# One-hot counting stage of a graph-attention kernel: register load, negation of x and the two score rows each put at another place

## The reference

```python
HW = h @ W
s = HW @ a[:512, 0];  t = HW @ a[512:, 0]
e = leaky_relu(s[row] + t[col], 0.2)          # row = src, col = dst
m = segment_max(e, row);  ex = exp(e - m[row])
att = ex / segment_sum(ex, row)[row]
agg = segment_sum(att[:, None] * h[col], row)
out = silu(agg) @ base_w.T + einsum(b_splines(agg), spline_w)
x = layernorm(x + out)
```

## The kernel before, in words

| windows | last tile | batch | group |
|---|---|---|---|
| 8, 9 | 67 | 8 | 5 |
| 10, 11 | 81 | 10 | 6 |
| 12, 13 | 94 | 11 | 7 |
| 14, 15 | 107 | 13 | 8 |
| 16, 17 | 121 | 15 | 9 |
| 18, 19 | 134 | 16 | 9 |
| 20, 21 | 147 | 18 | 10 |
| 22; 23; 24 | 153; 160; 166 | 19; 20; 20 | 11; 12; 12 |

## Time and profile before

### The profile page before, as it was taken

How to read it: one execution, slowest core, us unless ns; L and a number is a source line. 1 busy time by engine, 2 the same in 40 slices (tenths; PEclk the granted TensorE clock), 3 DMA queues, 4 the chain that set the end, 5 groups by cost and what they waited for, 6 DMA issues and landing times.

```text
span 384.6 us, 5446 instructions
## 1 busy us (share of the span) xinstructions
PE 370.0 (96%) x2082; PEld 304.6 (79%) x2082; DVE 336.8 (88%) x428; ACT 253.6 (66%) x252; POOL 37.1 (10%) x92
## 2 busy tenths in 40 slices
PE   7797899999999999999999999999999999999994
PEld 3676568888888888888888888888888888888883
DVE  8998799987764889999899997988999799999455
ACT  6769745445337979874876874896766696766122
POOL 6001301000000010101001010100100101010000
PEclk9999999999999999999999999999999999999999
DMA  7911987000000066577644546342343353453102
GB/s 253 399 23 40 221 147 217 2 2 0 2 0 0 2 208 179 168 239 219 179 151 149 180 119 203 117 109 56 114 128 88 104 146 109 154 192 111 55 27 109
DMA packets 23979, 47.28 MB, mean 123 GB/s; under 512 B 1936, under 2 KB 2412, under 8 KB 23954
## 3 DMA queue, kind: packets, MB, share of 16 engines
q0 software_dynamic: 12416, 24.00, 23.7%
q1 hardware_dynamic: 11538, 22.95, 18.4%
HBM read 44.37 MB, written 2.57 MB: 122 GB/s over the span
## 4 chain that ended last, share of the span: by engine, by line
PE 86%; DVE 8%; ACT 2%; issue 2%; POOL 1%; DVEq 1%; POOLq 0%
PE PS L1414 38%; PE PS L1410 25%; PE PS L1351 18%; PE PS L1333 3%; DVE oh L557 2%; DVE still L573 2%; PE PS L1361 1%; ACT C L1045 1%; DVE hit L536 1%; DVE oh L523 1%; ACT Z L1050 1%; PE PS L1424 0%; ACT xl L1055 0%; DVE pat L546 0%; DVEq L301 0%
## 5 line engine op out<-in xcount | busy, mean ns | idle before, releaser
L1414 PE MATMUL PS<-wh,s 128*128 128x512 f32 x432 | 139.4, 390 | 0.0
L1414 PEld LDWEIGHTS PS<-wh,s 128*128 128x128 f32 x432 | 81.2, 188 | 16.8
L1410 PE MATMUL PS<-s,wh 128*128 128x482 f32 x288 | 92.8, 383 | 0.0
L1414 PE MATMUL PS<-wl,s 128*128 128x512 f32 x216 | 84.2, 390 | 0.0
L1144 ACT ACTIVATE s<-v 128x1220 fp32r<-128x1220 f32 (+1 forms) x32 | 40.0, 1251 | 37.5 <-DVE v L932 26.3
L1410 PEld LDWEIGHTS PS<-s,wh 128*128 128x128 f32 x288 | 54.6, 189 | 9.7
L1127 ACT ACTIVATE v<-xt,bias 128x1220 f32<-128x1220 f32 (+1 forms) x32 | 42.9, 1341 | 20.1 <-DVE s L942 18.1
L1410 PE MATMUL PS<-s,wl 128*128 128x482 f32 x144 | 55.2, 384 | 0.0
L926 DVE SCALAR_TENSOR_TENSOR v<-v,v 128x1220 f32<-128x1220 f32 (+1 forms) x32 | 46.4, 1451 | 6.3 <-ACT v L1130 6.3
L932 DVE SCALAR_TENSOR_TENSOR v<-v,v 128x1220 f32<-128x1220 f32 (+1 forms) x32 | 46.8, 1461 | 3.3
L514 POOL DMA_DIRECT2D wh<-in_splT x32 | 23.0, 718 | 256.1 <-PE PS L1414 183.0
(11 more groups left out here) (162 smaller groups left out, 427.3 us busy)
## 6 DMA issues: line engine op xcount, KB each, us to landing
wh<-in_splT POOLq DMA_DIRECT2D x32, 512.0 KB, 4.2
wring<-in_splT SPq DMA_DIRECT2D x21, 512.0 KB, 4.5
xt<-in_xT SPq DMA_DIRECT2D x1, 2500.0 KB, 12.2
xh<-in_x POOLq DMA_DIRECT2D x1, 2304.0 KB, 11.8
wh<-in_baseT POOLq DMA_DIRECT2D x4, 512.0 KB, 5.5
out<-xr SPq DMA_DIRECT2D x8, 256.0 KB
wring<-in_baseT SPq DMA_DIRECT2D x3, 512.0 KB, 4.0
xr<-in_x SPq DMA_DIRECT2D x1, 1280.0 KB, 5.9
```

The lines of the kernel that those rows point to most:

```text
L1410: m = e.matmul(PS[:, w, 0:TURNED], wx[:, ic, 128 * w:128 * w + 128], sx[:, ic, 0:TURNED], start=begins, stop=ends_)
L1414: m = e.matmul(PS[:, out_bank(w), :], sx[:, ic, c:c + 128], wx[:, ic, :], start=begins, stop=ends_)
```

## The change

- `left_table` runs one group later, between `hits(9)` and `one_hot_still(9)`, and not behind `lanes(8)`. `LOADS_AT` becomes 9: DVE's five register loads stand behind the issue of `lanes(9)`, and PE's load behind group 9 and `s_column`.
- `minus_x(k)` runs at the end of batch 7 + k for all ten k.
- PE's `st_rows` parts stand behind groups 3 to 6, ACT's `st_rows` before the evacuation of batch 11.
- ACT's `s_part` stands before the evacuations at batch 17, not at its end.

```diff
-        LOADS_AT = 8
-        NEGATIVE_AT = {11 + k: k for k in range(NT - 3)}
+        LOADS_AT = 9
+        NEGATIVE_AT = {7 + k: k for k in range(NT)}
@@ vector
+                if g == 9:
+                    left_table()
                 one_hot_still(g)
...
-                if g == 8:
-                    left_table()
                 if g == LOADS_AT:
@@ scalar
-                if b == 13:
+                if b == 11:
                     st_rows()
+                if b == 17:
+                    e.wait_ge(s_sc, 4)
+                    for k, (lo, hi) in enumerate(TCH):
+                        e.mul(s_part[:, lo // 128:hi // 128], ...
                 for w, n in TAKEN:
                     if LAST_TILE[w + n - 1] // TB == b:
                         evacuate_counts(w, n)
...
                 if b in NEGATIVE_AT:
                     k = NEGATIVE_AT[b]
                     minus_x(k)
-                if b == 17:
-                    e.wait_ge(s_sc, 4)
-                    (the same s_part lines)
-            for k in range(len(NEGATIVE_AT), NT):
-                minus_x(k)
@@ tensor
-                if g in (4, 5, 6, 7):
-                    st_rows(g - 4)
+                if g in (3, 4, 5, 6):
+                    st_rows(g - 3)
```

More of the change, by code:

```diff
@@ L1061, in _ @@
                            PS[:, 6:8, 0:4].rearrange("p b (a c) -> p a b c", c=2)).then_inc(s_wa, 1)
-                if b == 13:
+                if b == 11:
                     st_rows()
+                if b == 17:
+                    e.wait_ge(s_sc, 4)
+                    for k, (lo, hi) in enumerate(TCH):
+                        e.mul(s_part[:, lo // 128:hi // 128],
+                              PS[:, 6 + k % 2, lo // 64:hi // 64].rearrange("p (j a) -> p j a", a=2)[:, :, 0], SLOPE - 1
+                              ).then_inc(s_scol, 1)
                 for w, n in TAKEN:
```

## The result

The changed kernel took 389.57 us (median of 20 runs), the kernel before 387.19 us (20 runs). The ratio is 1.0059, 95% interval 1.0046 to 1.0073: **slower by 0.6%**, where 0.4% faster was forecast. The forecast of 387.4 us was counted from a median of 3 runs, 388.95; against the 387.19 of 20 runs the same gain of 1.54 us would be 385.65. The profiled span is 386.8 us against 384.6. One run of the changed kernel took 397.5 us at a lower clock, and the ratio leaves it out.

The account below looks back on a forecast made before the run. PE bounds nearly everything behind the first 50 us; before that ACT sets the end. ACT's work, 16.48 us from 25.93, ends 1.54 us sooner: span 384.6 - 1.54 = 383.06, median 388.95 - 1.54 = 387.4 us, range 385.9 to 389.0.

Parts of the forecast that it names:

- the score rows and POOL's DMAs: SP's and POOL's transfers: ACT's `strow` copies end 3.3 us sooner, `gentle` lands at 40.2, and all `xl` parts have slack.
- Rival 3: SP's small stores and `gentle` get stuck behind `xl`; landing at 46.1 makes it 1.9 us slower, 390.9; chance 0.05.
- the used-up gain: `gentle` lands 3.9 us later than forecast, at 44.1, behind `xl`, and the gain is gone; chance 0.07.
- main case: ACT's last copy ends at 42.41 us, 1.54 us sooner, with no step waiting; span 383.06 us, time 387.4 us.
- The register load: On DVE, the load hides under `one_hot_still(9)` and `lanes(9)`, saving 1.5 us; on PE it costs 0 to 1.41 us.
- Rival 2: Loads not hidden: DVE pauses behind `lanes(9)`, gain 1.2 to 1.5 us, 387.6; chance 0.1, inside "same".
- ACT's sum: ACT's work from 25.93 us on, 16.48 us without waits, so the last copy ends at 42.41 against 43.95.
- rival 4: On ACT, `xh` comes at 23.5, pair 10, 11 starts 0.7 us late; gain 0.85 us, 388.1; chance 0.08.

Follow-up runs that it names:

- Experiment 6: The changed kernel with POOL's `xl` transfers held until the four stores of `strow` have landed: 384.90 us, ratio 0.9957 to the kernel before.
- experiment 1: The changed kernel with POOL's `xl` transfers held until `gentle` has landed: 385.16 us, ratio 0.9947 to the kernel before.
- experiment 4: The kernel before with only the register loads and `left_table` moved: 385.86 us, ratio 0.9970 to the kernel before.
- experiment 7: The kernel before with only the score rows and `s_part` moved: 386.96 us, ratio 1.0002 to the kernel before.
- experiment 2: The changed kernel with `minus_x` back at its old places, batches 11 to 17 and behind all batches: 384.98 us, ratio 0.9945 to the kernel before.
- experiment 5: The changed kernel with the `xl` transfers as plain copies in place of accumulations: 385.34 us, ratio 0.9977 to the kernel before.
- experiment 8: The changed kernel with POOL held until `gentle` has landed and only four `minus_x` early: 384.08 us, ratio 0.9925 to the kernel before.

## Why the prediction was wrong

- **The step that failed** is the one on the score rows and POOL's DMAs: "`gentle` is issued at 36.38 - 3.3 = 33.1, and lands at 40.2 by its 7.1 us", with the `xl` parts costed at nothing because PE reads them late. The question asked of the `xl` transfers was when they are needed, and not what they do to others in flight. In the changed kernel `gentle` was issued at 37.17 and landed at 46.43, 6.2 us later than forecast: some 4 us from the stores, the rest from its own transfer.
- **Rival 3 was the right mechanism**, at a chance of 0.05 (0.12 with the used-up gain). It named a landing at 46.1 as the price of 1.9 us; it was 46.43 and 2.4 us. What was held against it was `trow`'s 5.0 us beside an `xl` part. That row was misread. POOL's issue takes 1.35 us from 35.70, so `trow` (35.98) and `gentle` (36.38) were issued during it, and the queues show that the `xl` part moved nothing until 41.5: it ran behind them and not beside them, and that wait is also in its 13.0 us. The row showed what a transfer costs that goes first. Experiment 6 repeats that order, and it is harmless there too.
- **The rule on arbitration.** The Trainium skill (DMA: Bandwidth & Descriptors, the paragraph on arbitration) says that each DMA engine alternates between its queues packet by packet, and the prediction took that as support for the main case. By this case's runs it doesn't bound a small transfer's delay: four stores of 2 to 3 KB landed 4.6 us behind the end of the last issue, against 1.1 us on quiet engines, and from 37 to 40 us of the changed kernel 245 packets of one queue moved and none of the other, with `trow` issued. The measurement decides.
- **The register load.** That "the load can run while `one_hot_still(9)` and `lanes(9)` do" is right (31.4 in the changed kernel, hidden in experiments 1, 4 and 6). What failed is its duration: 1.41 us was taken as fixed. It was 4.54 and 4.93 us with the accumulation in flight. PE's load, bounded by 0 and 1.41 because "The trace has no row for it alone", does have a row in the trace before: 0.47 us; it is 1.11 in the changed kernel. Rival 2 had a pause of DVE behind `lanes(9)`, but from a load of 1.41 us that waits for an empty engine; no forecast case had a longer load. The longer loads cost 0.7 us of the last copy (43.14 against 42.41), hidden behind the later `gentle`.
- **ACT's sum** of 16.48 us held: experiment 6 ends at 42.4 with a span of 383.0 (forecast 383.06), ratio 0.9957. The row at 26.72 that gave the end of PE's last `st_rows` part, 27.5, is the part behind group 6, and that is where the last part now stands. `xh` came in time in the changed kernel (0.47 us of waiting before 22.08), so rival 4 didn't matter there; in experiment 1 it did.
- **What each part was worth**: loads alone -0.3%, rows alone 0, all parts without the early `minus_x` -0.55%. With it, +0.6%. The early `minus_x` is the part that turns the sign, and by way of POOL's transfer, not of ACT: the same early `minus_x` with the transfer held gives -0.5%.
- **What the clock adds to the medians.** The loads alone gave 1.2 us in the medians, where the stage shows about 0.7. Of the 17 executions of the kernel before that were measured beside it, 8 had spans of 384.5 to 384.6 us at a mean granted clock of 0.996 or more, and 9 had 385.1 to 386.3 at 0.989 to 0.994. Of the 12 with the loads moved, one was under 0.996, and ten had spans of 383.7 to 384.3. So the loads are worth some 0.6 us of span at the same clock, and the rest of the medians' difference goes with the lower clocks being rarer. With PE's 2.0 us of idle time ahead of group 9 the lower clocks came in 9 of 17, 13 of 29 and 5 of 10 executions (the kernel before twice, and experiment 7); with 0.43 to 0.44 us of it in 4 of 50 (experiments 1, 2, 4, 5, 6 and 8). That the idle time causes the fall is argued from these counts and from the one profile of experiment 7, not shown.

Open: why the accumulation holds up a register load that a faster plain transfer leaves alone, and what decides which queue's transfer goes first.

## What to carry to other kernels

When an edit makes some engine's work earlier, list which transfers that work releases, and lay them over every small latency-bound step of that time: tiny stores with a wait for landing, broadcasts, register loads. Large transfers with slack should be held until those are through; one wait on POOL was worth 1.1% here. A duration from a stretch with quiet DMA engines isn't the duration beside a large accumulation. And two transfers whose issue and landing overlap need not have run beside each other: look at what each queue moved before one is called harmless to the other.

## What the runs showed of the hardware

- A load of five registers on DVE took 1.41 us with quiet DMA engines (1.409 to 1.419 in seven kernels), 1.41 beside a plain transfer of 264 to 393 GB/s, and 4.54 and 4.93 us while an accumulating one moved some 200 GB/s; one register on PE took 0.47 us against 1.11 and 1.26. Where an accumulating part had been issued but moved nothing yet, PE's load stayed short (0.49 us at 36.7 in experiment 6, 0.47 in experiment 2).
- The load runs while the engine computes: it began at 31.4, when `one_hot_still(9)` had just started and `lanes(9)` was to come, and without the accumulation the comparison behind `lanes(9)` followed without a gap.
- An accumulating transfer into SBUF moved at about 205 GB/s with the DMA engines fully busy, a plain one of the same bytes at 393 (32 to 33 us of experiment 5).
- Two large transfers of SP's and POOL's queues ran mostly one behind the other: 0.94 MB of one and none of the other in 4 us of the kernel before, 0.48 MB and none in 3 us of the changed one.
- In the changed kernel PE's granted clock fell too, behind its idle time before 44.8, as this windows view shows; it was back at full before the transposes, which took their usual 0.87 us.

```profile
44.00:46.00 2.00, 1.20 (x3) 0.43 (x4) 1.22 (x3) 0.00 (x0) 0.00 (x0) 0.71 1.00 291
46.00:48.00 2.00, 2.00 (x6) 0.75 (x5) 1.64 (x5) 0.00 (x0) 0.00 (x0) 0.50 1.13 207
48.00:50.00 2.00, 2.00 (x10) 0.93 (x9) 1.51 (x9) 0.00 (x0) 0.00 (x0) 0.94 0.56 99
```
